# Attention stage: ScalarE copies projected Q and K to SBUF as f32, VectorE splits them from there; M and V2, V3 at other places in TensorE's order

## The chip, the cores and the metric

One core of a Trainium2 chip runs the whole program. The metric is the time of one execution in microseconds (us); 1718.09 us is the median of three runs of the kernel before (1714.54 to 1723.4). TensorE, VectorE, ScalarE, GpSimd and SP each run their own list of instructions in order and meet only at semaphores.

## The reference

The program is two transformer blocks on x of 16 x 512 x 128, f32. The change touches only the first stage, the causal attention:

```python
x = x + attn(layernorm(x))
# attn: 16 heads of 8, ALiBi slopes, no mask other than causal
qkv = einsum('btc,fc->btf', x, W_attn)
scores = q @ k.T * 8 ** -0.5 + slope * (key - query), -inf where key > query
y = softmax(scores) @ v;  out = y @ W_proj.T
```

Behind it stand the projection, an expert-choice feed-forward, a convolution and state-space mixer, and a feed-forward with 8 experts of which 2 count. They are the same in both kernels.

## The kernel before

The attention works batch by batch (16, `nb`), in four steps (`st`) of four heads (`g`). A batch's Q and K are made while the batch before is worked on. Q and K are each split into three bf16 parts, written to HBM as rows, and loaded back into the operand tiles `qop` and `kop`, where one product over 63 rows gives scores, ALiBi term and minus the maximum together.

Each step has, on TensorE:
- S0 to S5 (L430 to L442), scores with queries as rows, for the maxima. They go to two tiles `psS`, in turn; VectorE reduces each (L548).
- M (L472 to L478), which turns the last step's maxima, held as two bf16 parts in `mhl`, into rows, into one bank. ScalarE copies it to `mT` (L574), and SP's two DMAs (L283) put it into `qop`.
- E0 to E5 (L443 to L459), two units each: scores of two steps ago again, with keys as rows, minus the maximum. ScalarE's 12 exponentials (k = 0 to 11, L619) read them.
- V0 to V3 (L460 to L470): probabilities times V, into `psY`, copied by ScalarE (L600). V0 and V1 stand at the end of the step, V2 and V3 in the next step. They wait for GpSimd's masks 0 to 3 (`clear_future`, L344), which clear what lies in the future after exponentials 4, 8, 10 and 12.

The order of TensorE is written out in `ORDER` (L138). E units, M, the transposed x (X), the projected Q and K (step 0) and V (W, step 2) share three banks `psE` in a ring, in the order in which they are issued (`RING`, L163 to L174). Whoever writes to a bank waits for its last reader (`wait_ring`, L198).

Splitting: ScalarE writes the high part of Q or K, bf16, from the bank (`hi_part`, L576, after exponential 5 for Q and 9 for K, in step 0). VectorE subtracts it from the bank into `rest`, f32 (`split`, L510): for Q after reduction 3 of step 0, for K at the head of step 1. GpSimd makes the middle and the low part from `rest` (`split_rest`, L328), both ahead of mask 0 of step 1. SP writes the three parts to HBM (L288) in step 1; GpSimd issues the DMAs into `qop` (six, L223) at the head of step 2 and those into `kop` (three, L229) behind each of masks 0 and 1. The next batch's first instructions on TensorE wait for all of them (`s_op`). Layernorm for the batch after next is on VectorE in step 3. For the first batch (the head, ahead of the loop), VectorE makes all parts itself (L516 to L521).

`steps` (L235) runs batches 0 and 1 written out, the next twelve as a loop over pairs, and the last two written out.

Of the kernel before, what the change touches and what calls it, by code (L numbers as in the profile page):

```python
# [18 lines left out]
ALU = mybir.AluOpType  # L19
# [14 lines left out]
G = 4  # L34
# [32 lines left out]
def attention(nc, x_all, ident, x_in, w_attnT, qkv_scr, y_scr, rec_scr, pool_dma, shared, pj, pj_first, c_ident, c_identb, c_spread, c_maskq, c_rows, nb=NB):  # L67


    with ExitStack() as ctx:  # L70
# [43 lines left out]
        s_mr = sem("misc_ready")  # L114
        s_mf = sem("misc_free")
        s_rst = sem("rest_ready")
        s_hi = sem("hi_ready")
        s_mid = sem("mid_ready")
        s_lo = sem("lo_ready")
        s_sr = sem("scores_ready")  # L120
# [14 lines left out]
        e_units = [(j, p, h, 1 if j < 2 else 2) for j in range(TT) for h in ((0, 1) if j < 2 else (0,)) for p in range(2)]  # L135
        E_PAST = (4, 8, 10, 12)

        ORDER = ["S0", "E0", "S1", "E1", "M", "V2", "V3", "S2", "E2", "S3", "E3", "S4", "E4", "S5", "E5", "V0", "V1"]  # L138
        REST = 16 * (nb // 2 - 1)
        MISC0 = 4  # L140
        MISC = 2 * G
# [22 lines left out]
        for st in range(G):  # L164
            if st == 0:
                RING.append((st, "X"))
            for what in ORDER:
                before = {(0, "S3"): "Q", (0, "S5"): "K", (2, "S4"): "W"}
                if (st, what) in before:
                    RING.append((st, before[st, what]))  # L170
                if what == "M":
                    RING.append((st, "M"))
                if what[0] == "E":
                    RING += [(st, 2 * int(what[1]) + p) for p in range(2)]  # L174
# [23 lines left out]
        def wait_ring(eng, b, st, kind):  # L198

            at = RING.index((st, kind))  # L200
            older = [(b, k) for k in range(at - 3, -1, -3)]
            if not isinstance(b, int) or b > 0:
                older += [(b - 1, k) for k in range(len(RING) - 1, -1, -1) if k % 3 == at % 3]
            for bb, k in older:
                st_, kind_ = RING[k]
                if in_ring(bb, st_, kind_):
                    if isinstance(kind_, int):
                        eng.wait_ge(s_ex, EN * (G * bb + st_ - 2) + kind_ + 2)
                    elif kind_ in "QK":
                        eng.wait_ge(s_rst, 2 * bb + 3 + (kind_ == "K"))  # L210
                    else:
                        eng.wait_ge(s_mf, freed(bb, st_, kind_))
                    return
            eng.wait_ge(s_mf, FREE0)
            eng.wait_ge(s_rst, 2)

        ROWS = ((0, 3), (24, 2), (40, 1))

# [92 lines left out]
        @block.gpsimd  # L311
        def _(pool):
            pool.memset(mhalf[:], -0.5).then_inc(s_vinit, 1)
            pool.memset(zeros[:], 0.0).then_inc(s_vinit, 1)
            pool.wait_ge(s_vinit, 2)

            def clear_v(n):

                pool.memset(vaug[n][:], 0.0).then_inc(s_vinit, 1)
                pool.wait_ge(s_vinit, 2 * n + 3)  # L320
                pool.memset(vaug[n][:, :, :, D:2 * D], 1.0).then_inc(s_vinit, 1)

            def factors(b):
                pool.wait_ge(s_xn, b)
                pool.wait_ge(s_stat, 3 * b + 3)
                pool.tensor_tensor(rstd[:], veps[:], mhalf[:], ALU.pow).then_inc(s_rstd, 1)

            def split_rest(b, s):  # L328

                pool.wait_ge(s_rst, 2 * b + s + 1)  # L330
                if b == 2:
                    pool.wait_ge(s_first, 96 + 16 * 12)
                if b > 2:
                    pool.wait_ge(s_op, 16 * 12 * (b - 2))
                pool.tensor_tensor(parts[s][:, 1], rest[s][:], zeros[:], ALU.add).then_inc(s_mid, 1)
                pool.wait_ge(s_mid, 2 * b + s + 1)
                pool.tensor_tensor(parts[s][:, 2], rest[s][:], parts[s][:, 1], ALU.subtract).then_inc(s_lo, 1)

            def clear_future(u, j):

                if 0 <= u < G * nb:
                    pool.wait_ge(s_ex, 1 + EN * u + E_PAST[j])
                    diag = probs[u % 2][j][:, :, 0:P]
                    pool.affine_select(diag, diag, [[0, HG], [1, P]], ALU.is_ge, 0.0, base=0, channel_multiplier=-1).then_inc(s_msk, 1)  # L344

            for n in range(2):
                clear_v(n)
            factors(0)
            factors(1)
            for b in range(nb + 1):  # L350
                more = b + 1 < nb
                for st in range(G if b < nb else 2):
                    u = G * b + st - 2
                    if st == 1 and more:
                        for k in range(2):
                            split_rest(b + 1, k)
                    if st == 2 and more:
                        if b >= 1:
                            pool.wait_ge(s_er, EN * G * b)
                        pool.wait_ge(s_pw[0], 16 * b + 16)  # L360
                        for p in range(2):
                            place_q(pool, 1 - b % 2, s_op, p)
                    if st == 3 and b + 2 < nb:
                        factors(b + 2)
                    for j in range(TT):
                        clear_future(u, j)
                        if st == 2 and more and j < 2:
                            if j == 0:
                                pool.wait_ge(s_pw[1], 16 * b + 16)
                            place_k(pool, 1 - b % 2, s_op, j)  # L370

        @block.tensor
        def _(pe):
# [23 lines left out]
            def step(n, b, st, last):  # L397
# [11 lines left out]
                        wait_ring(pe, b, st, "X")  # L409
                        x_transposes(b + 1, ring_bank(st, "X"))  # L410
                    for what in ORDER:
                        if what == "S3" and st == 0 and not last:
                            wait_ring(pe, b, st, "Q")
                            pe.wait_ge(s_mf, freed(b, st, "X"))
                            project(0, ring_bank(st, "Q"))
# [66 lines left out]
        def _(dve):  # L482
# [24 lines left out]
            dve.wait_ge(s_first, 96)  # L507
            dve.tensor_scalar(wT[:, 0], wT[:, 0], D ** -0.5, None, ALU.mult).then_inc(s_yc, 1)

            def split(b, s, bank):  # L510
                dve.wait_ge(s_hi, 2 * b + s + 1)
                if not isinstance(b, int) or b:
                    dve.wait_ge(s_lo, 2 * b + s - 1)
                dve.tensor_tensor(rest[s][:], bank[:], parts[s][:, 0], ALU.subtract).then_inc(s_rst, 1)  # L514

            for s in range(2):  # L516
                split(0, s, psE[s])
                dve.wait_ge(s_rst, s + 1)
                dve.tensor_copy(parts[s][:, 1], rest[s][:]).then_inc(s_mid, 1)
                dve.wait_ge(s_mid, s + 1)  # L520
                dve.tensor_tensor(parts[s][:, 2], rest[s][:], parts[s][:, 1], ALU.subtract).then_inc(s_lo, 1)  # L521
# [3 lines left out]
            def step(n, b, st, last):  # L525
# [3 lines left out]
                if ahead:  # L529
                    dve.wait_ge(s_rest, REST)  # L530
                    norm_stats(b + 2)
                if st == 1 and not last:
                    split(b + 1, 1, ring_bank(0, "K"))
                if real and there(G * b + g - 1):
                    dve.wait_ge(s_hl, 2 * (G * b + g))
                for k in range(UN):
# [10 lines left out]
                            src = psS[k % 2][:, :, 0:2 * w].rearrange("p c (h k) -> p c h k", h=2)  # L547
                        dve.tensor_reduce(out, src, AX, ALU.max).then_inc(s_su, 1)  # L548
                    if k == 3 and st == 0 and not last:
                        split(b + 1, 0, ring_bank(0, "Q"))  # L550
                if real:
                    dve.wait_ge(s_su, 1 + UN * G * b + UN * (g + 1))
                    if there(G * b + st - 1):
# [10 lines left out]
        def _(act):  # L564
# [8 lines left out]
                    act.wait_ge(s_mrow, 32 * (G * b + st - 1))  # L573
                act.activation(mT[:], ring_bank(st, "M")[:].bitcast(BF16)[0:2 * HG, 0:T], ACT.Copy).then_inc(s_mf, 1)  # L574

            def hi_part(b, s, use, bank):  # L576
                act.wait_ge(s_mr, use + 1)
                if isinstance(b, int) and b == 1:
                    act.wait_ge(s_head, 48)
                elif not isinstance(b, int) or b:  # L580
                    act.wait_ge(s_pw[s], 16 * b - 16)
                act.activation(parts[s][:, 0], bank[:], ACT.Copy).then_inc(s_hi, 1)

            def copy_v(n, use, bank):
                act.wait_ge(s_mr, use + 1)
# [2 lines left out]

            copy_x(0, psY)
            for s in range(2):  # L590
                hi_part(0, s, s + 1, psE[s])
            act.wait_ge(s_vinit, 4)
            copy_v(0, 3, psE[2])
            act.activation(warm[:], ident[:, 0:1], ACT.Exp).then_inc(s_ex, 1)
# [7 lines left out]
            def step(n, b, st, last):  # L602
# [12 lines left out]
                for k in range(EN):  # L615
                    if there(u):
                        j, p, h0, nh = e_units[k]
                        act.wait_ge(s_er, EN * u + k + 1)
                        act.activation(probs[st % 2][j][:, 2 * p + h0:2 * p + h0 + nh, :].rearrange("p h q -> p (h q)"),  # L619
                                       ring_bank(st, k)[:, 0:nh * W[j]], ACT.Exp).then_inc(s_ex, 1)  # L620
                    if k == 3:
                        if there(G * b + st - 1):
                            copy_max(b, st, last)
                        if there(u) and there(u - 1):
                            copy_y(u - 1, st + 1)
                    if k == 5 and ahead:
                        hi_part(b + 1, 0, use_next(b, 1), ring_bank(0, "Q"))
                    if k == 9 and ahead:
                        hi_part(b + 1, 1, use_next(b, 2), ring_bank(0, "K"))
                    if k == 7 and st == 2 and not last:  # L630
                        if isinstance(b, int) and b == 0:
                            act.wait_ge(s_vinit, 6)
                        copy_v(1 - n, use_next(b, 3), ring_bank(2, "W"))
# [1620 lines left out]
```

## Time and profile before

| | before |
|---|---|
| median of the runs | 1718.09 us |
| profiled execution, its time | 1718.55 us |
| profiled execution, its span | 1716.7 us |
| attention stage | about 38 to 690 us of the span |
| mean granted TensorE clock | 0.836 of full |

The busy times over the whole span, from the head of the page:

```profile
PE 1226.1 (71%) x9530; PEld 728.2 (42%) x9531; DVE 1164.2 (68%) x3272; ACT 837.4 (49%) x2073; POOL 990.9 (58%) x1023
```

An engine's busy time is a mean over all stages. The attention stage is read from the waits, which say for each engine's instructions how long it stood and what it stood for, and from the timeline, where merged rows show the idle time ahead of them in brackets. A wait for several semaphores is put down to the last one.

### The profile page before, as it was taken

The numbers are of one execution on the slowest core, as the hardware profiler recorded it, in microseconds if no ns is written. First come the engines' busy times: TensorE is split into PE (matmuls) and PEld (weight loads), VectorE is DVE, ScalarE is ACT, GpSimd is POOL, SyncE is SP. The second block draws the span as 40 slices with busy tenths as digits, with TensorE's granted clock in tenths as the row PEclk, the third lists the DMA queues.
The fourth block names the chain that finished last, engine by engine and source line by source line (L and its number), as shares of the span: only waits on it lengthen the run. The fifth ranks groups of instructions, "written<-read, shape, count | busy, mean of one in ns | idle before, by whom it ended". The sixth has DMA issues, their size and how long they took to land. (4 is left out here: it accounts for less than half of the span.)

```text
span 1716.7 us, 35014 instructions
## 1 busy us (share of the span) xinstructions
PE 1226.1 (71%) x9530; PEld 728.2 (42%) x9531; DVE 1164.2 (68%) x3272; ACT 837.4 (49%) x2073; POOL 990.9 (58%) x1023
## 2 busy tenths in 40 slices
PE   2788788888777888584046366627099999999997
PEld 1334333433333433373035133327066655555555
DVE  2778687777666778386732499866866666666664
ACT  1567576766666677111212366634144444444443
POOL 1465455655454553241035399965268888888887
PEclk7899899999989999565568655655599999999999
DMA  4433333433322431362023200300423333333333
GB/s 112 144 82 92 73 105 90 96 88 93 77 71 77 95 96 62 116 222 73 0 85 73 68 26 25 118 6 24 181 38 41 42 42 43 41 41 42 41 43 40
DMA packets 88430, 125.49 MB, mean 73 GB/s; under 512 B 22434, under 2 KB 59106, under 8 KB 84242
## 3 DMA queue, kind: packets, MB, share of 16 engines
q0 software_dynamic: 41120, 45.22, 16.7%
q1 hardware_dynamic: 39170, 65.85, 11.5%
q10 hardware_dynamic: 8032, 12.93, 2.1%
q8 instruction: 74, 1.21, 0.3%
q14 instruction: 34, 0.28, 0.1%
HBM read 65.72 MB, written 57.68 MB: 72 GB/s over the span
## 5 line engine op out<-in xcount | busy, mean ns | idle before, releaser
L548 DVE TENSOR_REDUCE mx<-psS 128x2 f32<-128x768 f32 (+3 forms) x384 | 386.3, 1041 | 169.7 <-PE psS L441 169.0
L619 ACT ACTIVATE probs<-psE 128x512 f32<-128x512 f32 (+2 forms) x768 | 345.2, 523 | 162.4 <-PE psE L455 160.3
L344 POOL TENSOR_SCALAR_AFFINE_SELECT probs<-probs 128x512 f32<-128x512 f32 x256 | 162.1, 642 | 261.2 <-ACT probs L619 260.9
L2034 POOL DMA_INDIRECT out<-ex_y,ex_idx x144 | 236.7, 1644 | 47.5 <-issue 43.0
L455 PE MATMUL psE<-qop,kop 63*128 63x512 bf16 (+3 forms) x1024 | 195.5, 312 | 78.9 <-DVE rest L514 34.8
L467 PE MATMUL psY<-probs,vaug 128*32 128x512 f32 (+3 forms) x2048 | 180.8, 464 | 9.7 <-POOL probs L344 9.7
L2025 POOL DMA_INDIRECT ex_xg<-expert_tab,ex_idx x144 | 141.9, 985 | 66.0 <-issue 41.7
L2008 DVE SCALAR_TENSOR_TENSOR ex_h<-ex_psG,ex_w,ex_up 128x352 f32<-128x352 f32 x144 | 84.0, 584 | 106.1 <-PE ex_psG L2075 95.4
L441 PE MATMUL psS<-kop,qop 61*128 61x128 bf16 (+3 forms) x1024 | 141.8, 310 | 0.0
L2092 PE MATMUL ex_psY<-ah_w3s,ex_hT 128*128 (+1 forms) x864 | 133.2, 290 | 0.9 <-ACT ex_hT L2103 0.7
L455 PEld LDWEIGHTS psE<-qop,kop 63*128 63x128 bf16 x1024 | 65.1, 96 | 160.2 <-ACT probs L619 91.5
L436 PE MATMUL psS<-maskq,spread 64*128 64x128 bf16 (+2 forms) x1536 | 115.2, 227 | 19.9 <-DVE mx L548 19.8
L2102 ACT ACTIVATE ex_hT<-ex_psH 128x256 f32<-128x256 f32 x144 | 55.2, 383 | 135.5 <-PE ex_psH L2068 127.3
L2092 PEld LDWEIGHTS ex_psY<-ah_w3s,ex_hT 128*128 128x128 f32 (+1 forms) x864 | 107.6, 191 | 21.1 <-issue 3.5
L2074 PE MATMUL ex_psU<-ah_w1s,ex_xT 128*128 x288 | 110.1, 464 | 0.5 <-ACT ex_xT L2113 0.5
L436 PEld LDWEIGHTS psS<-maskq,spread 64*128 64x128 bf16 x1536 | 57.6, 96 | 122.6 <-DVE mx L548 84.9
L2075 PE MATMUL ex_psG<-ah_w2s,ex_xT 128*128 x288 | 109.3, 461 | 0.0
L467 PEld LDWEIGHTS psY<-probs,vaug 128*32 128x32 f32 x2048 | 69.4, 114 | 63.6 <-issue 31.3
L2113 ACT ACTIVATE ex_xT<-ex_psX 128x128 f32<-128x128 f32 x144 | 39.9, 277 | 107.3 <-PE ex_psX L2061 106.9
L2061 PE MATMUL ex_psX<-ident,ex_xg 128*128 128x128 f32 x144 | 47.6, 331 | 39.6 <-DMA ex_xg<-expert_tab,ex_idx 32.1
L2068 PE MATMUL ex_psH<-ident,ex_h 128*128 128x128 f32 (+1 forms) x432 | 72.2, 275 | 0.2 <-issue 0.2
L2107 ACT ACTIVATE ex_up<-ex_psU 128x352 f32<-128x352 f32 x144 | 66.7, 463 | 7.8 <-PE ex_psU L2074 0.8
(318 smaller groups left out, 2524.6 us busy)
## 6 DMA issues: line engine op xcount, KB each, us to landing
y_scr<-ysb SPq DMA_DIRECT2D x64, 256.0 KB, 3.1
qkv_scr<-parts SPq DMA_DIRECT2D x32, 384.0 KB, 3.2
qop<-qkv_scr POOLq DMA_DIRECT2D x30, 192.0 KB, 4.4
kop<-qkv_scr POOLq DMA_DIRECT2D x30, 192.0 KB, 5.9
expert_tab<-table_rows SPq DMA_DIRECT2D x1, 4352.0 KB, 13.1
pj_num<-y_scr SPq DMA_DIRECT2D x16, 256.0 KB
pj_rec<-rec_scr SPq DMA_DIRECT2D x16, 256.0 KB
x_scr<-x_all ACTq DMA_DIRECT2D x16, 256.0 KB, 3.3
```

What stands on the lines that cost most here:

```text
L344: pool.affine_select(diag, diag, [[0, HG], [1, P]], ALU.is_ge, 0.0, base=0, channel_multiplier=-1).then_inc(s_msk, 1)
L436: pe.matmul(out[:, :, P * j + lo:w], spread[rows, lo // HALF], maskq[rows, 0:nh, 0:P - lo], start=(lo == 0), stop=False, skip_group_check= ...
L441: mm = pe.matmul(out[:, h, :], half(qop[n], p, ROW_MAX)[:, hh, P * j:P * j + P], half(kop[n], p, ROW_MAX)[:, hh, 0:w], start=False, stop=( ...
L455: mm = pe.matmul(ring_bank(st, u)[:, W[j] * h:W[j] * h + W[j]], half(kop[m], p, ROW_END)[:, hh, P * j:P * j + P], half(qop[m], p, ROW_END) ...
L467: mm = pe.matmul(psY[32 * h:32 * h + 32, P * k:T], vaug[m_v][:, k, HG * e_v + h, :], probs[e_v % 2][k][:, h, :], start=(k == 0), stop=(k = ...
L548: dve.tensor_reduce(out, src, AX, ALU.max).then_inc(s_su, 1)
L619: act.activation(probs[st % 2][j][:, 2 * p + h0:2 * p + h0 + nh, :].rearrange("p h q -> p (h q)"), ring_bank(st, k)[:, 0:nh * W[j]], ACT.E ...
L2025: pool.indirect_dma_start(xg[t % 4][:], None, ytab, bass.IndirectOffsetOnAxis(ap=idx[t % 8][:], axis=0))\
L2034: pool.indirect_dma_start(out, bass.IndirectOffsetOnAxis(ap=idx[t % 8][:], axis=0), y[m][:], None, compute_op=ALU.add).then_inc(s_sc[m], 16)
L2074: pe.matmul(psU[n][:, 0:DE], xT[n][:], flat(w1s[:, e, :]), start=True, stop=True).then_inc(s_g2, 1)
L2075: pe.matmul(psG[n][:, 0:DE], xT[n][:], flat(w2s[:, e, :]), start=True, stop=True).then_inc(s_g, 1)
L2092: i = pe.matmul(psY[:, 0:C], hT[m][0:wd, f], flat(w3s[0:wd, f, e, :]), start=(f == 0), stop=(f == len(FC) - 1))
```

## The change

In step 0, ScalarE copies the bank of Q or K as f32 into `rest` and so frees it. VectorE then casts `rest` to the high part and subtracts that from `rest` in place. The copies stand after exponential 3 (Q) and 9 (K), the splits on VectorE after reduction 3 of step 0 (Q) and after reduction 2 of step 1 (K). The Q projection moves ahead of S2. `ORDER` puts M between E0 and S1, and V2, V3 between E2 and S3; so the copy of the maxima stands behind exponential 1 and that of y behind exponential 5. GpSimd splits Q ahead of mask 0 and K between masks 1 and 2 of step 1.

```diff
-        ORDER = ["S0", "E0", "S1", "E1", "M", "V2", "V3", "S2", "E2", "S3", "E3", "S4", "E4", "S5", "E5", "V0", "V1"]
+        ORDER = ["S0", "E0", "M", "S1", "E1", "S2", "E2", "V2", "V3", "S3", "E3", "S4", "E4", "S5", "E5", "V0", "V1"]
...
-                before = {(0, "S3"): "Q", (0, "S5"): "K", (2, "S4"): "W"}
+                before = {(0, "S2"): "Q", (0, "S5"): "K", (2, "S4"): "W"}
...
                     elif kind_ in "QK":
-                        eng.wait_ge(s_rst, 2 * bb + 3 + (kind_ == "K"))
+                        eng.wait_ge(s_raw, 2 * bb + 3 + (kind_ == "K"))
...
             def split_rest(b, s):
 
-                pool.wait_ge(s_rst, 2 * b + s + 1)
+                pool.wait_ge(s_rst, 4 * b + 2 * s + 2)
...
                     if st == 1 and more:
-                        for k in range(2):
-                            split_rest(b + 1, k)
+                        split_rest(b + 1, 0)
...
                     for j in range(TT):
+                        if st == 1 and more and j == 2:
+                            split_rest(b + 1, 1)
                         clear_future(u, j)
...
-                        if what == "S3" and st == 0 and not last:
+                        if what == "S2" and st == 0 and not last:
...
-            def split(b, s, bank):
-                dve.wait_ge(s_hi, 2 * b + s + 1)
-                if not isinstance(b, int) or b:
-                    dve.wait_ge(s_lo, 2 * b + s - 1)
-                dve.tensor_tensor(rest[s][:], bank[:], parts[s][:, 0], ALU.subtract).then_inc(s_rst, 1)
+            def split(b, s):
+                dve.wait_ge(s_raw, 2 * b + s + 1)
+                if isinstance(b, int) and b == 1:
+                    dve.wait_ge(s_head, 48)
+                elif not isinstance(b, int) or b:
+                    dve.wait_ge(s_pw[s], 16 * b - 16)
+                dve.tensor_copy(parts[s][:, 0], rest[s][:]).then_inc(s_rst, 1)
+                dve.wait_ge(s_rst, 4 * b + 2 * s + 1)
+                dve.tensor_tensor(rest[s][:], rest[s][:], parts[s][:, 0], ALU.subtract).then_inc(s_rst, 1)
...
-                if st == 1 and not last:
-                    split(b + 1, 1, ring_bank(0, "K"))
...
                     if k == 3 and st == 0 and not last:
-                        split(b + 1, 0, ring_bank(0, "Q"))
+                        split(b + 1, 0)
+                    if k == 2 and st == 1 and not last:
+                        split(b + 1, 1)
...
-            def hi_part(b, s, use, bank):
+            def copy_raw(b, s, use, bank):
                 act.wait_ge(s_mr, use + 1)
-                if isinstance(b, int) and b == 1:
-                    act.wait_ge(s_head, 48)
-                elif not isinstance(b, int) or b:
-                    act.wait_ge(s_pw[s], 16 * b - 16)
-                act.activation(parts[s][:, 0], bank[:], ACT.Copy).then_inc(s_hi, 1)
+                if not isinstance(b, int) or b:
+                    act.wait_ge(s_lo, 2 * b + s - 1)
+                act.activation(rest[s][:], bank[:], ACT.Copy).then_inc(s_raw, 1)
...
-                    if k == 3:
-                        if there(G * b + st - 1):
-                            copy_max(b, st, last)
-                        if there(u) and there(u - 1):
-                            copy_y(u - 1, st + 1)
-                    if k == 5 and ahead:
-                        hi_part(b + 1, 0, use_next(b, 1), ring_bank(0, "Q"))
+                    if k == 1 and there(G * b + st - 1):
+                        copy_max(b, st, last)
+                    if k == 3 and ahead:
+                        copy_raw(b + 1, 0, use_next(b, 1), ring_bank(0, "Q"))
+                    if k == 5 and there(u) and there(u - 1):
+                        copy_y(u - 1, st + 1)
                     if k == 9 and ahead:
-                        hi_part(b + 1, 1, use_next(b, 2), ring_bank(0, "K"))
+                        copy_raw(b + 1, 1, use_next(b, 2), ring_bank(0, "K"))
```

## Rows read from the trace of the kernel before

**Rows 1.** Waits of 38 to 690 us: engine, line, releaser: total us, times, longest.
```profile
ACT probs L619 <- PE psE L455: 160.3, 89, 11.9
...
PE psE L455 <- DVE rest L514: 34.8, 28, 1.4
...
PE psE L455 <- DMA qop<-mT: 16.4, 12, 4.9
```

**Rows 2.** Timeline, TensorE's rows: start us, us, engine, line, operation, [idle before <-releaser].
```profile
316.94 0.34 PE L436 MATMUL psS<-maskq,spread 64*128 64x256 bf16 x4
...
320.27 1.13 PE L384 MATMUL psE<-xT,wT 128*128 128x512 f32 x2
...
327.03 0.34 PE L436 MATMUL psS<-maskq,spread 64*128 64x256 bf16 x4
...
328.77 0.47 PE L455 MATMUL psE<-qop,kop 63*128 63x512 bf16 x2 [1.29 <-DVE rest L514]
...
336.17 0.34 PE L436 MATMUL psS<-maskq,spread 64*128 64x256 bf16 x4
...
343.32 1.71 PE L467 MATMUL psY<-probs,vaug 128*32 128x512 f32 x16
...
344.96 0.34 PE L436 MATMUL psS<-maskq,spread 64*128 64x256 bf16 x4
```

**Rows 3.** Timeline, ScalarE, 314 to 346 us.
```profile
321.53 0.60 ACT L582 ACTIVATE parts<-psE 128x512 bf16<-128x512 f32 x1 [0.18 <-PE psE L384]
...
323.83 1.08 ACT L619 ACTIVATE probs<-psE 128x512 f32<-128x512 f32 x2 [0.94 <-PE psE L455]
...
329.19 2.06 ACT L619 ACTIVATE probs<-psE 128x512 f32<-128x512 f32 x4 [3.04 <-PE psE L455]
...
332.07 3.23 ACT L619 ACTIVATE probs<-psE 128x384 f32<-128x384 f32 x8
336.87 2.06 ACT L619 ACTIVATE probs<-psE 128x512 f32<-128x512 f32 x4 [1.57 <-PE psE L455]
```

**Rows 4.** VectorE: timeline of head and batch, then L514's durations, and the page's L548.
```profile
13.90 0.43 DVE L519 CAST parts<-rest 128x512 bf16<-128x512 f32 x1
...
14.37 0.69 DVE L521 TENSOR_TENSOR parts<-rest,parts 128x512 bf16<-128x512 f32 x1
...
306.44 0.48 DVE L556 CAST mhl<-mx 128x16 bf16<-128x16 f32 x1
...
326.74 0.17 DVE L556 CAST mhl<-mx 128x16 bf16<-128x16 f32 x1
326.95 1.16 DVE L558 TENSOR_TENSOR mhl<-mx,mhl 128x16 bf16<-128x16 f32 x1
...
L514 DVE TENSOR_TENSOR rest<-psE,parts x32: 676/680/690, 13.2 to 620.6; 128x512 f32<-128x512 f32 x32
...
L548 DVE TENSOR_REDUCE mx<-psS 128x2 f32<-128x768 f32 (+3 forms) x384 | 386.3, 1041 | 169.7 <-PE psS L441 169.0
```

**Rows 5.** GpSimd: timeline of two batches, then the landing times of its `kop` DMAs.
```profile
304.00 1.65 POOL L229 DMA_DIRECT2D kop<-qkv_scr  x3
305.63 1.25 POOL L344 TENSOR_SCALAR_AFFINE_SELECT probs<-probs 128x512 f32<-128x512 f32 x2
...
326.82 1.26 POOL L335 TENSOR_TENSOR parts<-rest,zeros 128x512 bf16<-128x512 f32 x1
...
336.28 3.13 POOL L223 DMA_DIRECT2D qop<-qkv_scr  x6 [0.25 <-issue]
...
340.01 1.70 POOL L229 DMA_DIRECT2D kop<-qkv_scr  x3
...
DMA to landing us min/median/max: 2.1/6.1/9.5
```

**Rows 6.** Timeline, SP's queue, 324.8 to 356 us.
```profile
333.15 0.94 SPq L288 DMA_DIRECT2D qkv_scr<-parts  x2
```

**Rows 7.** The page's DMA issues: what, KB each, us to landing.
```profile
qkv_scr<-parts SPq DMA_DIRECT2D x32, 384.0 KB, 3.2
```

More of the change, by code:

```diff
@@ L116, in attention @@
         s_rst = sem("rest_ready")
-        s_hi = sem("hi_ready")
+        s_raw = sem("raw_copied")
         s_mid = sem("mid_ready")
@@ L214, in wait_ring @@
             eng.wait_ge(s_mf, FREE0)
-            eng.wait_ge(s_rst, 2)
+            eng.wait_ge(s_raw, 2)
         ROWS = ((0, 3), (24, 2), (40, 1))
@@ L508, in _ @@
             dve.tensor_scalar(wT[:, 0], wT[:, 0], D ** -0.5, None, ALU.mult).then_inc(s_yc, 1)
-            def split(b, s, bank):
-                dve.wait_ge(s_hi, 2 * b + s + 1)
-                if not isinstance(b, int) or b:
-                    dve.wait_ge(s_lo, 2 * b + s - 1)
-                dve.tensor_tensor(rest[s][:], bank[:], parts[s][:, 0], ALU.subtract).then_inc(s_rst, 1)
+            def split(b, s):
[7 more added lines that the diff above has]
+                dve.tensor_tensor(rest[s][:], rest[s][:], parts[s][:, 0], ALU.subtract).then_inc(s_rst, 1)
             for s in range(2):
-                split(0, s, psE[s])
-                dve.wait_ge(s_rst, s + 1)
+                split(0, s)
+                dve.wait_ge(s_rst, 2 * s + 2)
                 dve.tensor_copy(parts[s][:, 1], rest[s][:]).then_inc(s_mid, 1)
@@ L590, in _ @@
             for s in range(2):
-                hi_part(0, s, s + 1, psE[s])
+                copy_raw(0, s, s + 1, psE[s])
             act.wait_ge(s_vinit, 4)
```

## The prediction, made before the changed kernel had run

> **What bounds the kernel now.** I read the waits of the attention stage first. The reader is to see that ScalarE's exponentials wait for TensorE 160 us in all, and that TensorE in turn waits 34.8 us (28 times) for VectorE's `rest` and 16.4 us (12 times) for the DMA that puts the turned maxima into `qop` [rows 1]. Then the timelines of one batch, by step. The first score unit S0 of the steps begins at 316.94, 327.03, 336.17 and 344.96 us: 10.09, 9.14 and 8.79 us for steps 0, 1 and 2 [rows 2]. In step 2 nothing of `rest` disturbs: ScalarE starts at 336.87, 0.70 us after S0, and has idled 1.57 us before it [rows 3]. This idle time is a loop: TensorE gets its last bank of a step from an exponential, then runs V0 and V1 (1.71 us [rows 2]), S0 and the first exponential's scores, and only then has ScalarE work. So the path goes through ScalarE's instructions up to its third last exponentials, and through TensorE's order around the step's end. VectorE and GpSimd lie beside it until something on TensorE waits for them.
>
> **What the change removes.** Today the bank of projected Q (and K) comes free only when VectorE has subtracted. TensorE stands 1.24 us each time on the mean [rows 1], 1.29 us in step 1 [rows 2]. On ScalarE, where the path is, that shows as 0.94 us idle ahead of exponential 8 of step 0, and 3.04 instead of 1.57 us at the head of step 1 [rows 3]: 0.94 + 1.47 = 2.41 us a batch, in 14 batches (28 waits, two each), 33.7 us. After the change ScalarE's own copy frees the bank. That copy is as long as now (0.60 us, the same shape read; f32 out instead of bf16: the exponentials write f32 and take 0.515, so I take 0).
>
> Step 1's 1.47 us is all on the path: K's copy ends well before the step, the two exponential units start 0.3 us after S0 as in step 2. 14 x 1.47 = 20.6 us.
>
> Step 0's 0.94 us is not all to be had, since TensorE is full there. I walk it from S0 = 0 with the spacing of step 2: exponentials of 512 columns 0.515 us apart, shorter ones 0.4 (four in 2.06, eight in 3.23 [rows 3]), copies about 0.5, a projection 1.13 [rows 2]. Exponentials 0, 1 at 0.71, 1.23; max copy 1.6; exponentials 2, 3 at 2.1, 2.6; the Q projection now waits for the max copy's bank (2.2) and ends 3.35, copy of Q at 3.4 (some 0.2 late, as the 0.18 today [rows 3]); exponentials 4, 5 at 3.9, 4.3; V2, V3 run 3.9 to 4.8, so the y copy is at 4.85; 6 to 9 at 5.3 to 6.7; the K projection waits for exponential 7 (6.2), ends 7.35, copy 7.4; exponentials 10, 11 at 7.9, 8.2; V0, V1 from 7.85, next S0 at 9.5. That is 0.59 us under 10.09: 14 x 0.59 = 8.2 us.
>
> **What it moves.** Turning the maxima (M) goes ahead of S1, so the max copy follows exponential 1 instead of 3: two exponentials, 1.0 us, earlier, and with it SP's two `qop` DMAs. The 12 waits of 16.4 us [rows 1] can shrink by 1.0 us each, 12 at most; at worst none, because K's write to HBM now comes from SP just ahead of them. I take half, 6 us. V2 and V3 after E2 instead of after E1 want their masks later than now; the y copy follows exponential 5. In steps without a projection the same walk gives exponential 6 at 4.4 us after S0 either way: 0, bounds 0 and 0.15 us a step.
>
> **What it adds.** VectorE now does a cast (0.43 us, with the next instruction 0.47 later) and a subtraction of two SBUF tiles (0.69) [rows 4] instead of one subtraction from PSUM (0.68): +0.47 us each, 28 times. It has six reductions of 1.04 us, 6.2 us, in a step of 8 to 9.5 [rows 4], so its sum fits. Its lateness does not: its last maxima of a step go to M, which now stands second on TensorE, with S1, E1 and every later matmul behind it. M wants them at 0.7 us after S0, ScalarE wants the turned maxima at 1.6; before, M had until about 2.3.
>
> And there is the port. Today the `mhl` subtraction at 326.95 takes 1.16 us instead of 0.17 and ends with GpSimd's instruction of 326.82 to 328.08; a cast at 306.44 takes 0.48 beside a mask [rows 4, 5]. The subtraction from PSUM is 676 to 690 ns in all 32 cases [rows 4], never disturbed. The new cast and subtraction have their operands in SBUF as the disturbed ones have. In step 0: reduction 3 ends 6.05, the cast runs to 6.5, a mask stands in GpSimd's queue for exponential 7 and takes its 0.63 (two in 1.25 [rows 5]), the subtraction is over 7.8, reductions 4 and 5 at 9.0 and 10.2. GpSimd starts splitting Q at 9.3 (two instructions, 1.26 and 1.16). The `mhl` cast at 10.3 then waits for the first, its subtraction perhaps for the second: ready between 10.6 and 12.1, that is 1.1 to 2.6 us after step 1's S0. M needs 0.3 more, ScalarE wants it at 1.6: a loss of 0 to 1.4 us. I take 0.9, nearer the end where both collide. In step 1 the K split is behind reduction 2, and the maxima are ready at 1.0 to 1.5 us of step 2: 0 to 0.6 us, I take 0.2.
>
> The Trainium skill, SBUF — State Buffer, on the shared port pair, says that a VectorE copy in a two-port mode, or an operation with two SBUF inputs against a GpSimd operation that reads SBUF, excludes GpSimd for the whole instruction, while one with an input in PSUM does not. The trace agrees (1.16 and 0.48 against 676 to 690 ns). By it the new split is exposed and the old was not, which is the second rival below.
>
> **GpSimd and the queues.** K's split moves from before mask 0 of step 1 to between masks 1 and 2. Masks 0, 1 come sooner (they waited behind four instructions from 326.82 on [rows 5]); K's split ends at about 8.4 us of step 1, the masks 2, 3 at 2.0 of step 2. The six `qop` DMAs then start at 2.0 instead of 0.1 (336.28), the two `kop` groups at 5.9 and 8.2 instead of 3.8 and 6.1 (the first at 340.01; it lasts 1.70 and a mask of 0.63 stands behind it [rows 5]). Mask 1 of step 2 stands between these and is over at 8.2, while V1 wants it at 8.0: I take 0.2 us, bounds 0 and 0.6. SP writes K at 0.8 of step 2 instead of with Q 3 us before it (333.15 [rows 6]); with 3.2 us to landing [rows 7] it is there near 4, in time for 5.9. The second `kop` group was 12.9 us ahead of the next batch's S0 (304.00, 316.94 [rows 2, 5]); now 10.8 less what is gained, against a landing of 6.1, at most 9.5 us [rows 5], after the third issue 1.1 us on: 0 in most batches.
>
> **Sum.** Per batch: -1.47 - 0.59 + 0.9 + 0.2 + 0.2 = -0.76; x 14 = -10.6. Maximum rows -6. The head does two splits in a row ahead of the first `kop` load: +0.9; batch 0, with no exponentials to gain from, +0.5. In all -15.2. The profiled execution took 1718.55 us (span 1716.7), 0.5 above the median of the runs, 1718.09; so 1703 us.
>
> **Rivals.**
> *A, forecast:* M partly late. Own range 1696 to 1710. Chance 0.42.
> *B, maxima in time.* GpSimd's instruction falls elsewhere, M never waits: -2.06 x 14 = -28.8, maximum rows -8, head and batch 0 +1.4: 1683 (1677 to 1695). For it: in the rows a VectorE instruction sometimes slips in ahead (the cast at 326.74 took 0.17). Against: the new split makes VectorE later by 0.47 just where GpSimd starts. Chance 0.23.
> *C, the bank wait turned into a wait for maxima.* 1.4 in step 1, 0.6 in step 2, 0.2 for V1: +0.14 x 14 = 2.0, with -6 and +1.4: 1716, no change. For it: the 1.16 of the row. Chance 0.18.
> *D, slower: GpSimd's chain for K.* Place: S0 of the next batch behind the last `kop` landing. If K's write lands 2 us late in the busy queues, the second group goes at 10.2 of step 2, its last DMA at 11.3, and lands at the 9.5 of the longest at 20.8. S0 is wanted at about 17.8 (8.8 and some 9): 3.0 us a batch, 42 in all, on top of A's -15: 1745; it decides from a second group later than about 9 us with the longest landing. With the median landing (17.4) it costs nothing, which speaks against it; a span of partial cases gives 1728 to 1745. Chance 0.13.
> Other: 0.04.
>
> A measurement of this kernel tells 0.5% (8.6 us) from no change. Faster than 1709.5: 0.88 of A, all of B, some rest: 0.62. Slower than 1726.7: D and a little of C: 0.16. Within: 0.22. The range from 1681 to 1723 leaves out the low end of B and most of D.
>
> **What would show it.** In the changed profile: no TensorE wait for `rest`; ScalarE's idle time ahead of step 1's first exponential back to about 1.6; the waits for `mhl` at M new, near 1 us in step 1 (A), absent (B) or over 1.4 and in step 2 as well (C); the new cast or subtraction, or the masks beside them, longer than 0.43, 0.69 and 0.64; the DMA waits at step 3 fewer and shorter; SP's K write in step 2; in D a wait of over 2 us ahead of the transposes of each batch. The prediction is wrong in mechanism if step 1's head does not shrink, or if V1 waits for masks by more than 0.6.

## The result and the profile after

The changed kernel takes 1709.79 us (median of 11 runs, 1703.58 to 1719.15), the kernel before 1717.34 (11 runs, 1713.24 to 1725.03). The ratio is 0.9957, 95% interval 0.9937 to 0.9977: 0.4% faster, where 1703 us, 0.9% faster, was forecast. The profiled execution took 1709.79 us, its span 1707.7.

The waits of the attention stage, 38 to 690 us, in the profile after (total us, times, longest):

```profile
ACT probs L622 <- PE psE L456: 130.0, 65, 13.2
...
PE psE L456 <- DMA qop<-mT: 23.7, 14, 2.1
...
PE psS L437 <- DVE mx L551: 13.1, 28, 1.2
...
PE psE L477 <- DVE mhl L563: 10.0, 18, 1.4
```

The wait for `rest` is gone, as is its 34.8 us [rows 1]. In its place TensorE waits 23.7 us for the maximum rows, where it was 16.4, and 10.0 us for `mhl`, which is new. Before, two of the 12 row waits were long (4.9 and 3.8 us) and the other ten 0.2 to 1.3; now 13 of the 14 lie between 1.5 and 2.1 us.

TensorE's rows in one batch, the answer to [rows 2]; S0 of steps 0, 1 and 2 at 310.81, 320.33, 328.90:

```profile
310.81 0.34 PE L437 MATMUL psS<-maskq,spread 64*128 64x256 bf16 x4
...
320.33 0.34 PE L437 MATMUL psS<-maskq,spread 64*128 64x256 bf16 x4
...
326.74 0.26 PE L437 MATMUL psS<-maskq,spread 64*128 64x128 bf16 x4 [0.52 <-DVE mx L551]
...
328.90 0.34 PE L437 MATMUL psS<-maskq,spread 64*128 64x256 bf16 x4
...
330.09 0.38 PE L477 MATMUL psE<-identb,mhl 128*8 128x128 bf16 x4 [0.52 <-DVE mhl L563]
...
339.98 0.58 PE L456 MATMUL psE<-qop,kop 63*128 63x512 bf16 x2 [1.76 <-DMA qop<-mT]
```

ScalarE's rows of steps 1 to 3 [rows 3]:

```profile
321.03 1.09 ACT L622 ACTIVATE probs<-psE 128x512 f32<-128x512 f32 x2 [1.58 <-PE psE L456]
322.25 0.59 ACT L579 ACTIVATE mT<-psE 8x512 bf16<-8x512 bf16 x1
...
325.30 2.73 ACT L622 ACTIVATE probs<-psE 128x384 f32<-128x384 f32 x6
329.61 1.08 ACT L622 ACTIVATE probs<-psE 128x512 f32<-128x512 f32 x2 [1.58 <-PE psE L456]
...
340.41 1.08 ACT L622 ACTIVATE probs<-psE 128x512 f32<-128x512 f32 x2 [3.50 <-PE psE L456]
```

The head of step 1 is back at 1.58 us of idle time (3.04 before). But from there to the next step's head it is now 8.58 us (321.03 to 329.61), where it was 7.68.

I take the S0 rows of all batches and subtract. Medians over batches 1 to 14 in us, with the sum over these batches in brackets; step 3 runs to the next batch's S0 and holds the loop's turn:

| kernel | step 0 | step 1 | step 2 | step 3 | wait for rows | ratio to before (95%) |
|---|---|---|---|---|---|---|
| before | 10.09 (144.7) | 9.13 (130.5) | 8.80 (133.1) | 10.84 (161.4) | 16.4 | |
| changed | 9.51 (134.6) | 8.58 (120.0) | 8.86 (134.9) | 11.53 (164.3) | 23.7 | 0.9957 (0.9937-0.9977) |
| raw_only | 9.22 | 9.23 | 8.80 | 10.93 | 16.0 | 0.9955 (0.9939-0.9972) |
| order_only | 10.59 | 9.37 | 8.68 | 9.55 | 3.6 | 0.9966 (0.9953-0.9979) |
| k_early | 9.52 | 9.92 | 8.68 | 9.59 | 4.9 | 0.9902 (0.9886-0.9917) |
| m_late | 9.55 | 8.17 | 8.72 | 13.51 | 37.9 | 1.0006 (0.9984-1.0028) |
| k_write_act | 9.52 | 8.58 | 9.41 | 9.68 | 7.4 | 0.9865 (0.9827-0.9902) |
| k_write_behind | 9.52 | 8.58 | 14.93 | 9.70 | 0 | 1.0334 (1.0285-1.0384) |
| k_early0 | 9.52 | 8.62 | 8.67 | 9.52 | 1.3 | 0.9802 (0.9766-0.9838) |
| k_mid | 9.52 | 9.10 | 8.68 | 10.12 | 10.7 | 0.9863 (0.9829-0.9897) |
| raw_k0 | 9.23 | 8.62 | 8.80 | 10.91 | 11.4 | 0.9928 (0.9903-0.9953) |
| k0_m_late | 9.55 | 8.62 | 8.73 | 10.94 | 23.8 | 0.9896 (0.9858-0.9935) |
| k0_q_old | 9.73 | 8.62 | 8.68 | 9.53 | 1.4 | 0.9833 (0.9791-0.9875) |
| k0_pool_waits | 9.52 | 9.82 | 8.68 | 9.53 | 2.5 | 0.9904 (0.9881-0.9927) |

(The medians of the runs below belong to four groups with their own runs of before, 1714.9 to 1720.7 us in the median, so the ratios are what to compare.)

The change gives 10.1 and 10.5 us in steps 0 and 1, and takes 1.8 in step 2 and 2.9 in step 3, although step 3 of before held two long waits (4.9 and 3.8 us) that are not there after; by the medians step 3 grew by 0.69 us. The attention stage is 15.7 us shorter in this profile (its last S0 at 655.0 against 670.7 us), the stages behind it, whose code is the same, 6.7 us longer (1052.7 against 1046.0; 1043.8 to 1050.3 in the twelve other kernels). TensorE's mean granted clock behind the attention stage was 0.762 after and 0.774 before; raw_k0, next in length with 1050.3 us, had 0.763. That points to the clock of the one execution, but whether these 6.7 us belong to it or to the change was not tested.

Why the rows come late is to be looked for in the DMA queues. SP's after, from step 1 to step 2, and the page's time to landing of the writes of Q's and K's parts (3.2 before [rows 7]):

```profile
322.87 1.30 SPq L283 DMA_DIRECT2D qop<-mT  x2
324.30 5.45 SPq L288 DMA_DIRECT2D qkv_scr<-parts  x2
329.95 0.35 SPq L296 DMA_DIRECT2D y_scr<-ysb  x1
331.21 1.33 SPq L283 DMA_DIRECT2D qop<-mT  x2
...
qkv_scr<-parts SPq DMA_DIRECT2D x32, 384.0 KB, 2.6
```

SP issues the rows at 331.21, 2.3 us after step 2's S0 (3.2 before), as planned. But K's write, started with Q's in one row at 333.15 before [rows 6], 2.5 us ahead of step 2, now goes out at the end of the 5.45 us row, at about 329.4, and y's behind it. Both are issued in front of the rows. The rows are there at 339.9, 8.7 us after their issue. GpSimd's side [rows 5]:

```profile
320.12 1.26 POOL L335 TENSOR_TENSOR parts<-rest,zeros 128x512 bf16<-128x512 f32 x1
...
328.19 1.16 POOL L337 TENSOR_TENSOR parts<-rest,parts 128x512 bf16<-128x512 f32 x1
...
330.47 3.15 POOL L223 DMA_DIRECT2D qop<-qkv_scr  x6
...
334.21 1.69 POOL L229 DMA_DIRECT2D kop<-qkv_scr  x3
...
336.49 1.64 POOL L229 DMA_DIRECT2D kop<-qkv_scr  x3
```

`qop`'s loads start 1.6 us into step 2 (0.1 before), `kop`'s at 5.3 and 7.6.

The traces also hold the semaphore updates with which each DMA ends. From them, medians over batches 1 to 14, in us from step 2's S0 (negative: in step 1):

| kernel | K's write landed | y's write landed | `qop` loads start | `kop` loads start | rows issued | rows landed |
|---|---|---|---|---|---|---|
| before | 0.7 | 1.4 | 0.1 | 3.8 | 3.2 | 10.0 |
| changed | 3.0 | 3.7 | 1.6 | 5.3 | 2.3 | 10.95 |
| k_early0 | -0.1 | 1.1 | -0.2 | 3.9 | 2.3 | 9.0 |
| k_mid | 1.0 | 1.7 | 0.1 | 3.9 | 2.3 | 9.9 |
| k_write_act | 5.9 | -1.1 | 1.6 | 6.2 | 2.3 | 10.0 |
| k_write_behind | 10.7 | -1.0 | 1.6 | 11.0 | 2.3 | 9.5 |

In steps 0 and 1, where GpSimd has no loads running, the same two DMAs land 2.4 us after their issue, in every kernel; in step 2 they take 6.1 to 8.7 us in all fourteen. So most of the 8.7 us is spent beside GpSimd's loads, before as after. K's and y's writes had landed 0.7 and 1.4 us after the rows' issue in the changed kernel, 7 us ahead of the rows.

### The profile page after: what moved, and what is told of

The parts are those of the page before. It is cut to its first block and busy times, and to the rows that moved or that the text cites. A ratio compares the mean times of both kernels' runs of the same rounds, so it can differ in the third digit from the quotient of the medians.

```text
span 1707.7 us, 35056 instructions
## 1 busy us (share of the span) xinstructions
PE 1230.7 (72%) x9528; PEld 723.2 (42%) x9531; DVE 1187.3 (70%) x3304; ACT 850.4 (50%) x2073; POOL 991.2 (58%) x1023
## 5 line engine op out<-in xcount | busy, mean ns | idle before, releaser
L622 ACT ACTIVATE probs<-psE 128x512 f32<-128x512 f32 (+2 forms) x768 | 351.7, 523 | 133.4 <-PE psE L456 130.0
L456 PE MATMUL psE<-qop,kop 63*128 63x512 bf16 (+3 forms) x1024 | 187.3, 311 | 56.6 <-ACT probs L622 28.8
L468 PE MATMUL psY<-probs,vaug 128*32 128x512 f32 (+3 forms) x2048 | 169.8, 450 | 10.3 <-POOL probs L344 10.3
L468 PEld LDWEIGHTS psY<-probs,vaug 128*32 128x32 f32 x2048 | 54.4, 111 | 83.7 <-issue 45.4
```

The lines of the kernel that those rows point to most:

```text
L456: mm = pe.matmul(ring_bank(st, u)[:, W[j] * h:W[j] * h + W[j]], half(kop[m], p, ROW_END)[:, hh, P * j:P * j + P], half(qop[m], p, ROW_END) ...
L468: mm = pe.matmul(psY[32 * h:32 * h + 32, P * k:T], vaug[m_v][:, k, HG * e_v + h, :], probs[e_v % 2][k][:, h, :], start=(k == 0), stop=(k = ...
```

## The experiments

Theory L: the gain is lost because K's parts are made and written late, so that K's write and the loads stand in front of the maximum rows. Rivals: a shorter batch must pay in step 3, since the loads are bound by their amount (S); M's early place is itself the loss (M).

**raw_only** takes the copies and SBUF splits into the old order, K's split at the head of step 1 and GpSimd's both ahead of mask 0:

```diff
-        ORDER = ["S0", "E0", "M", "S1", "E1", "S2", "E2", "V2", "V3", ...
+        ORDER = ["S0", "E0", "S1", "E1", "M", "V2", "V3", "S2", "E2", ...
...
+                if st == 1 and not last:
+                    split(b + 1, 1)
                 if real and there(G * b + g - 1):
```

> Only the copies are changed: ScalarE copies Q (after exponential 5) and K (after 9) as f32, VectorE splits from SBUF (Q after reduction 3 of step 0, K at the head of step 1), GpSimd splits both ahead of mask 0, and TensorE's order is the old one. Theory L (the changed kernel gives its gain back because K's parts are written 5 us later, so K's write and the operand loads stand in front of the maximum rows): here K is written early, step 3 keeps its old lengths (typical waits for the rows 0 to 1.3 us), step 0 is about 0.6 and step 1 about 1.3 us shorter than before: some 26 us less than before, 1688 to 1700. Rival S (the loads are bound by their amount, so any shortening of steps 0 and 1 comes back as a wait in step 3): step 3 grows by over 1 us a batch, 1707 to 1714.

1712.15 us: not the time of L, and in the range of S, but not for S's reason. Step 3 did stay (10.93), step 0 fell by more than expected, step 1 did not fall at all. Its waits:

```profile
PE psS L436 <- DVE mx L552: 46.9, 75, 1.5
...
PE psE L455 <- DMA qop<-mT: 16.0, 10, 4.3
```

TensorE now waits 46.9 us for VectorE's reductions (19.8 before), 28.8 of it in step 1: the split ahead of reduction 0 holds up S2 and everything behind it. VectorE is what binds step 1, which neither theory had.

**order_only** is the kernel before with the new `ORDER`, the maximum copy behind exponential 1 and y's behind 5.

> The kernel before with only the new order: M between E0 and S1, V2 and V3 between E2 and S3, the maximum copy after exponential 1 and the y copy after 5; the bank is still freed by VectorE. Theory L: the rows are issued 1.0 us earlier with K's write in its old place, so the waits of step 3 fall by 0.5 to 1 us a batch, and M waits up to 1 us in step 1: 1706 to 1716. Rival M (M's early place is itself a loss, because of the wait for VectorE's maxima): 1717 to 1727.

1714.38 us, as L has it. The rows' waits fell from 16.4 to 3.6, step 3 from 10.84 to 9.55; steps 0 and 1 grew by 0.50 and 0.24, with the bank's wait as it was:

```profile
PE psE L455 <- DVE rest L514: 34.8, 28, 1.4
...
PE psE L455 <- DMA qop<-mT: 3.6, 5, 1.4
```

Here the rows' earlier issue works, with K written in its old place. The wait of up to 1 us at M in step 1 that was expected did not come: M stands there 2.1 us after S0, behind E0's wait for `rest`, and finds the maxima ready. Rival M falls as a loss by itself, but it has a price in steps 0 and 1.

**k_early** is the changed kernel with K's split at the head of step 1, GpSimd's ahead of mask 0 (the second part of the diff above).

> The changed kernel with K's split back at the head of step 1 on VectorE and both splits ahead of mask 0 on GpSimd, so that K is written with Q; all else as changed. Theory L: waits for the maximum rows in step 3 fall from 1.5 to 2.1 us to under 0.7, step 3 shortens by 1 to 1.5 us a batch, 1688 to 1700. Rival S: the waits stay over 1.3 us, 1706 to 1713.

1704.28 us, a ratio of 0.9902, slower than L's 1700. But the waits fell from 23.7 to 4.9 us and step 3 to 9.59, which is L's mechanism and not S. Step 1 grew to 9.4 to 10.7 us. VectorE at its head:

```profile
320.72 0.17 DVE L562 TENSOR_TENSOR mhl<-mx,mhl 128x16 bf16<-128x16 f32 x1
320.88 1.31 DVE L516 CAST parts<-rest 128x512 bf16<-128x512 f32 x1
322.23 0.69 DVE L518 TENSOR_TENSOR rest<-rest,parts 128x512 f32<-128x512 f32 x1
322.84 5.81 DVE L552 TENSOR_REDUCE mx<-psS 128x4 f32<-128x512 f32 x6
```

The cast of K takes 1.31 us instead of 0.42 (GpSimd's second split instruction runs from 320.73 to 321.91), and no reduction starts before 322.84. TensorE's S2 waits for the first:

```profile
323.58 0.26 PE L436 MATMUL psS<-maskq,spread 64*128 64x128 bf16 x4 [1.47 <-DVE mx L552]
```

**m_late** moves M behind E1 again in the changed kernel (`"S1", "E1", "M", "S2"`), its copy behind exponential 3.

> The changed kernel with M back behind E1 and its copy after exponential 3 (V2, V3 stay behind E2). Theory L (the rows stand behind K's write and the loads, wherever M is): rows issued about 1 us later land less than 1 us later, step 3's wait grows by 0.3 to 1 us; M no longer waits for the maxima (0.5 us in step 2, 0.3 in step 1 saved): 1706 to 1716. Rival M (M's wait costs the gain): 1700 to 1706, with step 3 as in the changed kernel.

1722.42 us, no change against before, slower than L expected and far from M: step 1 shorter by 0.41 us, step 3 longer by 1.98 (a wait longer by 0.3 to 1 was expected).

```profile
PE psE L456 <- DMA qop<-mT: 37.9, 14, 3.9
```

The rows were issued 0.9 us later, landed 0.6 us later (11.6 us into step 2) and cost 14 us more in waits, 1.0 us a batch. What else makes step 3 longer here was not followed up. M's own wait is worth 0.4 + 0.14 us a batch, less than what its early place brings.

**k_write_act** and **k_write_behind** leave all splits where the change put them and move only K's write:

```diff
-                    for k in range(2):
+                    for k in range(1):
                         sp.wait_ge(s_lo, 2 * b + k + 3)
...
+                    if k == 1 and st == 2 and not last:
+                        act.wait_ge(s_lo, 2 * b + 4)
+                        act.dma_start(qkv_scr[1 - n, 1].rearrange("a p q -> p a q"), parts[1][:]).then_inc(s_pw[1], 16)
```

(k_write_behind has these two instructions on SP, behind the rows of step 2.)

> The changed kernel, K's write of 384 KB issued by ScalarE after the maximum copy of step 2 instead of by SP; splits and order as changed. Theory F (the maximum rows are late because they stand behind K's write in SP's own queue): waits in step 3 fall from 1.5 to 2.1 us to under 0.6, ScalarE loses some 0.5 us a batch to the issue, 1688 to 1700. Rival C (the 16 DMA engines are full, whoever issues): the waits stay over 1.3 us, 1708 to 1718.

> The changed kernel, K's write still on SP but behind the two maximum-row DMAs of step 2. Theory F: the waits for the rows in step 3 vanish (under 0.5 us), though the kop loads now wait for K's write and V1 for mask 1, up to 1 us a batch: 1695 to 1712. Rival C: rows' waits stay over 1.3 us in step 3 and the masks' wait comes on top: 1712 to 1730.

k_write_act: 1691.53 us, the waits 7.4 us (9 times), step 3 9.68, and 0.55 us more in step 2:

```profile
PE psE L456 <- DMA qop<-mT: 7.4, 9, 2.8
```

K's write is still the earlier one, by half a microsecond, but in another queue:

```profile
322.52 0.37 ACTq L628 DMA_DIRECT2D qkv_scr<-parts  x1
...
323.04 1.33 SPq L283 DMA_DIRECT2D qop<-mT  x2
```

The 0.55 us are not the issue on ScalarE: its exponentials stand as in the changed kernel. GpSimd waits for K's write to land, mask 1 stands behind its loads, and V1 behind mask 1:

```profile
327.55 1.69 POOL L229 DMA_DIRECT2D kop<-qkv_scr  x3 [1.45 <-DMA qkv_scr<-parts]
...
329.94 0.85 PE L468 MATMUL psY<-probs,vaug 128*32 128x384 f32 x8 [0.91 <-POOL probs L344]
```

The rows landed 10.0 us into step 2 instead of 10.95, with `qop`'s loads where they were. So about 1 us of their lateness goes with K's write leaving SP's queue, as F has it; the longer step 2, which asks for the rows 0.55 us later, takes off the rest of the wait. Since `kop`'s loads start 0.9 us later too, and y's write goes out in step 1 again, F and C are not fully parted.

k_write_behind: 1773.11 us, outside both expectations. No wait for the rows is left, but that is no sign for F: the rows landed at 9.5, and step 2 now lasts 14.9 us. The price of K being late was far more than expected, because the write itself took 7.1 us to land (6.9 in the median):

```profile
323.36 0.39 SPq L291 DMA_DIRECT2D qkv_scr<-parts  x1
...
330.52 1.70 POOL L229 DMA_DIRECT2D kop<-qkv_scr  x3 [5.66 <-DMA qkv_scr<-parts]
...
332.93 1.51 PE L471 MATMUL psY<-probs,vaug 128*32 128x384 f32 x8 [5.13 <-POOL probs L347]
```

GpSimd stands 5.66 us for it, mask 1 stands behind GpSimd's loads, and V1 waits 5.13 us; such waits are 84.7 us in all (10.3 in the changed kernel, a single one). This is the chain of rival D, at mask 1 and not at the next batch's S0. In the changed kernel K's write landed at 3.0 us of step 2 and the first `kop` loads started at 5.3: 2.3 us to spare.

**k_early0** has K's split behind reduction 0 of step 1 (`if k == 0 and st == 1`), GpSimd's both ahead of mask 0. **k_mid** has it behind reduction 1 and GpSimd's between masks 0 and 1.

> The kernel k_early with K's split on VectorE after reduction 0 of step 1 instead of at its head; GpSimd splits both ahead of mask 0. Theory P (k_early's step 1 is 9.4 to 10.5 us because the split stands ahead of reduction 0 and is held up by GpSimd's instructions on the shared port, so S2 and all behind it wait): step 1 shortens to 8.6 to 9.3 us, 1695 to 1703. Rival B (VectorE is simply full in step 1, wherever the split stands): step 1 stays over 9.4, 1702 to 1708.

> The changed kernel with K's split on VectorE after reduction 1 of step 1 and GpSimd's between masks 0 and 1: K is written some 2 us earlier than in the changed kernel. Theory F and C alike: rows' waits in step 3 fall by about half or more, to under 1 us; step 1 stays 8.5 to 8.9: 1694 to 1704. If the waits don't move with the write's time, both fall: 1706 to 1712.

k_early0 takes 1682.79 us, 2.0% under before: faster than both kernels, and than its expectation. Step 1 is 8.62, step 3 9.52, and the waits are:

```profile
PE psS L436 <- DVE mx L550: 30.1, 67, 1.8
...
PE psE L455 <- DMA qop<-mT: 1.3, 4, 0.4
```

K is written with Q again, in step 1 (S0 at 309.49):

```profile
313.46 2.34 SPq L288 DMA_DIRECT2D qkv_scr<-parts  x2
```

k_mid: 1693.38 us; K's write some 2 us sooner than in the changed kernel, the waits 10.7 instead of 23.7. Step 1 was 9.10, longer than expected. Here K's and y's writes had landed (1.0 and 1.7 us) before the rows were issued (2.3), and the rows still landed at 9.9, where k_early0 has 9.0. So a late K delays the rows even when nothing stands ahead of them in SP's queue; that points to GpSimd's loads, which start 0.3 us later here and 1.8 later in the changed kernel. Which share is the write's and which the loads' no run separates.

**raw_k0** (raw_only with K's split behind reduction 0), **k0_m_late** (k_early0 with M behind E1) and **k0_q_old** (k_early0 with Q's projection ahead of S3 again, its copy behind exponential 5) take k_early0 apart.

> raw_only with K's split on VectorE behind reduction 0 of step 1 instead of at its head: the copies and splits of k_early0, TensorE's order the old one. Theory P (raw_only's step 1 stayed at 9.2 us because the split stands ahead of reduction 0): step 1 shortens to 8.0 to 8.7, step 0 stays 9.2, step 3 keeps its waits for the rows (near 1 us a batch): 1692 to 1704, a ratio of 0.985 to 0.993. If the new order has no part in k_early0's gain: the ratio of k_early0, 0.980.

> k_early0 with M back behind E1 and the maximum copy behind exponential 3. With K's write early, the rows land in time up to about 1 us of lateness: step 3 grows by 0.5 to 1 us a batch against k_early0, steps 0 to 2 change by under 0.3 each: a ratio of 0.983 to 0.990. Rival: the place of M is free once K is early: 0.978 to 0.982.

> k_early0 with Q's projection back ahead of S3 and its copy behind exponential 5 (M, V2, V3 as changed). In raw_only, with Q there, step 0 is 9.22 us against 9.52 in the kernels with the new order. If Q's early place costs these 0.3 us: step 0 9.2, 4 us in all, a ratio of 0.976 to 0.979. If it is M's and V2's place that costs them: step 0 9.5 or more, 0.980 to 0.984.

raw_k0 1704.39, k0_m_late 1698.9, k0_q_old 1685.64 us. The ratios of the first two are as expected: the copies and splits alone are 0.7%, the new order on top another 1.3%; with M late 0.9% goes, in step 3 (10.94, more than expected). In k0_q_old step 0 is 9.73: Q's early place is no loss, and the 0.3 us by which raw_only's step 0 is shorter belong to the order of M, V2 and V3. With M alone moved back step 0 stays at 9.55, which speaks for V2 and V3.

**k0_pool_waits** adds one wait to k_early0, on GpSimd:

```diff
                     if st == 1 and more:
+                        pool.wait_ge(s_hl, 2 * G * b + 2)
                         for k in range(2):
                             split_rest(b + 1, k)
```

> k_early0 with one wait more on GpSimd: ahead of splitting Q in step 1 it waits until VectorE has made both parts of step 0's maxima. Theory of the port (VectorE's mhl cast takes 0.72 instead of 0.17 us because GpSimd's first split instruction has begun): the cast is back at 0.17 to 0.2 us, VectorE's reductions of step 1 begin some 0.5 us sooner after S0, GpSimd's split begins some 0.5 us later; the time falls by 0 to 6 us, a ratio of 0.976 to 0.981. Rival (the cast is long for another reason, such as its own data or SBUF writes of ScalarE): it stays over 0.5 us. Either way under 0.2 us a step is lost by masks that come later.

1698.1 us, a ratio of 0.9904: the mechanism right, the time wrong. VectorE at the head of step 1 in k_early0:

```profile
309.85 0.72 DVE L560 CAST mhl<-mx 128x16 bf16<-128x16 f32 x1
...
311.42 0.66 DVE L516 CAST parts<-rest 128x512 bf16<-128x512 f32 x1
312.12 0.69 DVE L518 TENSOR_TENSOR rest<-rest,parts 128x512 f32<-128x512 f32 x1
```

and in k0_pool_waits:

```profile
316.98 0.17 DVE L561 CAST mhl<-mx 128x16 bf16<-128x16 f32 x1
...
318.01 0.99 DVE L517 CAST parts<-rest 128x512 bf16<-128x512 f32 x1
319.04 1.53 DVE L519 TENSOR_TENSOR rest<-rest,parts 128x512 f32<-128x512 f32 x1
```

The `mhl` cast is back at 0.17 us. But GpSimd's two instructions (317.45 to 320.02) now fall on K's split, whose cast takes 0.99 and whose subtraction 1.53 us, and step 1 grows by 1.2 us. The collision moved to a costlier place.

## Why the prediction was right, and where not

- Step 0: forecast 9.5 us, measured 9.51; the walk by spacings held, the shared walk of Q's copy included (0.36 us idle ahead of it, 0.2 forecast).
- Step 1: net -0.57 us forecast (-1.47 + 0.9), -0.55 measured. The first part is exact (3.04 to 1.58 us idle). The 0.9 is right in size and half wrong in cause. The port was there, with one instruction and not two: the `mhl` cast took 0.72 us beside GpSimd's of 320.12, M waited 0.75 us (k0_pool_waits, with `mhl` in time, has it 0.55 us sooner), and ScalarE's copy behind it came about 0.2 us late. The rest is S5's wait for reduction 3, 0.52 us at 326.74, behind K's split. I had costed that split as fitting into VectorE's sum and had looked only at its last maxima.

VectorE's rows for both, to be compared with [rows 4]:

```profile
316.82 0.42 DVE L517 CAST parts<-rest 128x512 bf16<-128x512 f32 x1
317.27 1.03 DVE L519 TENSOR_TENSOR rest<-rest,parts 128x512 f32<-128x512 f32 x1
...
320.69 0.72 DVE L561 CAST mhl<-mx 128x16 bf16<-128x16 f32 x1
...
324.68 0.42 DVE L517 CAST parts<-rest 128x512 bf16<-128x512 f32 x1
325.12 0.69 DVE L519 TENSOR_TENSOR rest<-rest,parts 128x512 f32<-128x512 f32 x1
...
329.41 0.55 DVE L563 TENSOR_TENSOR mhl<-mx,mhl 128x16 bf16<-128x16 f32 x1
```

- The same rows bear out the port: the new subtraction takes 1.03 us at 317.27 beside mask 1 and 0.69 where nothing runs; the subtraction from PSUM never took longer. The sentence drawn from the Trainium skill (SBUF — State Buffer, on the shared port pair, which the one that starts first keeps for its whole instruction) agrees with this and with k0_pool_waits; in all these rows it is VectorE that waits for GpSimd.
- Step 2: M waits 0.52 us for `mhl`, whose subtraction takes 0.55 beside GpSimd, yet the step grew by 0.06 where 0.4 was forecast. V1 waited for no mask: the loads started at 1.6, not 2.0. Priced too high, 4.8 us in all.
- The maximum rows are the step that failed. "12 at most; at worst none, because K's write to HBM now comes from SP just ahead of them. I take half, 6 us": their waits grew by 7.3 us, outside both bounds. I had named K's write and given its price as a gain not made. It is a loss: the rows go out 0.9 us sooner and land 1.0 us later. With K split earlier they land in time or nearly so (waits of 3.6 us in order_only, 4.9 in k_early, 1.3 in k_early0), and k_mid stands between. The cause as far as it is shown is the late splitting of K, which moves its write and GpSimd's loads; the share of SP's queue is at most about 1.4 us of the 8.7 (k_write_behind). The bound of 12 was also too high: six of the 12 waits before were shorter than 1.0 us, so that 9.2 was the most. Over the 14 batches step 3 grew by 2.9 us, or 0.69 a batch by the medians; the two long waits of before hide the difference.
- The head: 0.7 us later (0.9 forecast). Batch 0, from S0 to S0, 35.7 us against 36.9, where +0.5 was forecast.
- The sum. In the profiled executions the attention stage became 15.7 us shorter, and -15.2 was forecast: the lost row term (8.9 us in step 3) was made up by step 2, batch 0, and steps 0 and 1, whose sums fell by 10.1 and 10.5 where 14 times the medians gives 8.1 and 7.7 (a few long steps of before are not there after). That agreement is partly luck. The time fell by 8.8 us in these two executions and by 7.5 between the medians of 11, half of the forecast; what separates it from 15.7 lies, in the profiled pair, behind the attention stage. The stated range, 1681 to 1723 us, holds the time of the kernel before as well, so that the time lay in it says little.
- Rival D did not come, but its margin was small: 2.3 us at mask 1, as k_write_behind shows.

## To carry to other kernels

Freeing a bank sooner is worth only what the engine that took over the work leaves of it: ask which wait that engine ends next, and whether it ends it later. When a producer moves later by some microseconds, follow its DMA and the loads that wait for it, ask which small transfers run beside them, and price their lateness as a loss, not as a gain missed. Here much the same copies were worth 0.4%, 1.4% or 2.0%, by where one split and one write stood.

## What the hardware showed that I had not expected

- Two small DMAs (4 KB each) landed 2.4 us after their issue with no loads running, and 6.1 to 8.7 us after it (medians of fourteen kernels) beside GpSimd's loads of `qop` and `kop`. In the changed kernel, the one with 8.7, the 384 KB write ahead of them in the same queue had landed 0.7 us after their issue.
- The same 384 KB write landed 3.2 us after its issue on the median of before, and 7.1 us when it was issued into the running loads.
- An instruction on VectorE with its operands in SBUF took 0.17, 0.31 or 0.72 us, or 0.42, 0.66, 0.99 and 1.31, by what GpSimd had begun; taking one collision away made a costlier one.
